# The step-by-step scan of layer 1 moved into array tiles of 32, with its row layout made by DMA

## The chip, the cores and the metric

One program runs on one core of a Trainium2 chip. The metric is the device time of one execution in microseconds, lower is better. Times in a profile are counted from the start of its span.

## The reference

Two layers work on x of 2 batches x 1024 tokens x 256. Layer 0 is a linear attention and a sparse feed-forward; neither is touched here. Layer 1 is a scan and a mixture of eight experts. What is computed in layer 1:

```
h = layernorm(x) * (1 + ca) + sa
k, v = h @ Wk.T, h @ Wv.T            # 16 heads of 16 wide, k gets a rotation by position
for each minibatch of 16 tokens:     # 64 of them, per batch and head; W starts as the identity
    z = k W;   W = W - k.T (z - v) * 2/(16*16)
x = x + ga * (layernorm(z) * gamma + beta) @ Wo.T
h = layernorm(x) * (1 + cb) + sb
gates = softmax of the two largest of h @ gate_w, 0 for the other six experts
x = x + gb * (sum_e gates_e * expert_e(h) + shared(h))
```

The minibatches follow one another: each z needs the W that the last gradient left. The expert biases b2 and the shared bias are added as one product of the gates (with a ninth column of ones) and b2.

## The kernel before, in words

Every engine has its instruction order written out by hand; semaphores say what waits for what. The phases are attention, feed-forward, scan (`scan_phase`) and mixture (`moe_phase`); all engines meet at the end of each.

**Scan.** A chunk is 128 tokens of both batches (`NC` = 8 chunks), and a chunk has `NMB` = 8 steps of 16 tokens. A batch has 256 channels in `KD` = 2 halves of 8 heads, so there are four units, one for each batch and half, each with a W of 128 x 128 that is masked to its diagonal blocks. In a step, for each batch:

1. z: TensorE adds k W into the rows of the step in `z_ps` (line 1545). `k_diag` holds k turned, with zeros around the 16 columns of each step, so that the product has 128 rows and only 16 of them are not zero.
2. u: VectorE takes v - z for all 128 tokens (line 1403).
3. gradient: TensorE adds k.T u to `g_ps` (line 1554). `k_rows` holds k once for each step, with the other rows set to zero; ACT makes these copies (`spread`, line 1254).
4. w: VectorE multiplies `g_ps` by `head_blocks`, the mask times 2/256 (`new_w`, line 1374).

Both batches are in every step, batch 0 first on each engine. In 32-bit float each matrix product is two loads of weights and two matmuls in the profile, which are called records below.

Around the steps stand pieces for the next and the last chunk, each at a fixed place: on TensorE (`filler`) the turning of the normalized x, of k and of z, the projection to k and v (3 pieces for each batch, line 1480), and the output rows (line 1488); on VectorE the norms, the split of h in a high and a low part (`split`, lines 1353 and 1355), the rotation (lines 1365 and 1367), and the gating of the output rows (line 1349). ACT drains turned tiles and keeps v and z; POOL sums the rotation (line 1209), adds to x (line 1214) and computes 1/sqrt. The last chunk also has the norms and the split of the mixture's first group of 512 tokens (lines 204, 220, 1593, 1595).

Behind the last step come the statistics of z (line 1337), its centring, turning and output rows, and then the mixture.

**Mixture.** Four groups of 512 tokens. For each, 16 matmuls of 8 columns give the logits (line 1791), VectorE picks the top two, TensorE turns the gates (line 1798), which have nine columns, and for each tile of 128 tokens come the product of nine rows of gates with b2 (line 1819), the shared products (line 1821) and eight expert products (line 1833), which VectorE adds up one by one (line 1754). The hidden layer of the next group (line 1808) stands between them.

## Time and profile before

| what | us |
|---|---|
| median of 3 runs | 1100.81 (1100.41 to 1100.9) |
| profiled execution, its own time | 1098.78 |
| its span | 1097.0 |
| from the end of the feed-forward to the scan's first product | 712.3 to 722.2 |
| the scan's 64 steps | 722.2 to 918.5 |
| from the last u to the mixture | 918.5 to 929.5 |
| the mixture | 929.5 to 1097.0 |
| TensorE busy | 1019.1 (93%) |
| VectorE busy | 733.8 (67%) |

The profile is of one execution. Its own time and its span differ by what lies before the first and behind the last instruction. PE is TensorE's matmuls, PEld its loads of weights, DVE is VectorE; a queue's name has a q at its end.

### The profile page before, as it was taken

The numbers are of one execution on the slowest core, as the hardware profiler recorded it, in microseconds if no ns is written. First come the engines' busy times: TensorE is split into PE (matmuls) and PEld (weight loads), VectorE is DVE, ScalarE is ACT, GpSimd is POOL, SyncE is SP. The second block draws the span as 40 slices with busy tenths as digits, with TensorE's granted clock in tenths as the row PEclk, the third lists the DMA queues.
The fourth block names the chain that finished last, engine by engine and source line by source line (L and its number), as shares of the span: only waits on it lengthen the run. The fifth ranks groups of instructions, "written<-read, shape, count | busy, mean of one in ns | idle before, by whom it ended". The sixth has DMA issues, their size and how long they took to land. (4 is left out here: it accounts for less than half of the span.)

```text
span 1097.0 us, 15610 instructions
## 1 busy us (share of the span) xinstructions
PE 1019.1 (93%) x5736; PEld 850.5 (78%) x5736; DVE 733.8 (67%) x1657; ACT 380.9 (35%) x731; POOL 227.2 (21%) x284
## 2 busy tenths in 40 slices
PE   6899999999999999998699999888999887999997
PEld 5688888888888888887588888667777775877775
DVE  7766667666666676666569866577878775466456
ACT  4334333333434333333133222044455433421220
POOL 2222222222222221222110011132222224111011
PEclk9999999999999999999999999999999998999999
DMA  9300000000000000000130000030000000000000
GB/s 302 110 1 1 1 1 1 1 1 1 1 1 1 1 1 1 1 1 16 33 100 1 1 1 1 0 98 0 0 0 0 1 2 1 1 15 15 10 20 19
DMA packets 19058, 20.91 MB, mean 19 GB/s; under 512 B 4905, under 2 KB 14898, under 8 KB 18994
## 3 DMA queue, kind: packets, MB, share of 16 engines
q1 hardware_dynamic: 18994, 20.05, 5.6%
q8 instruction: 41, 0.67, 0.3%
q14 instruction: 23, 0.19, 0.1%
HBM read 17.95 MB, written 2.10 MB: 18 GB/s over the span
## 5 line engine op out<-in xcount | busy, mean ns | idle before, releaser
L393 POOL TENSOR_TENSOR rope_sum<-rope_cos,rope_sin 128x512 f32<-128x512 f32 x80 | 115.0, 1437 | 257.0 <-DVE rope_sin L514 257.0
L429 ACT ACTIVATE rope_exp<-rope_sum 128x512 f32<-128x512 f32 x80 | 50.5, 631 | 205.7 <-POOL rope_sum L393 205.6
L783 PE MATMUL proj<-wo_sb,attn_out_t 128*128 128x256 f32 x512 | 113.2, 379 | 0.7 <-issue 0.7
L783 PEld LDWEIGHTS proj<-wo_sb,attn_out_t 128*128 128x128 f32 x512 | 96.1, 190 | 13.4 <-issue 0.9
L732 PE MATMUL num<-v_ones,score_masked 128*128 128x129 f32 x512 | 100.2, 278 | 5.9 <-DVE score_masked L572 5.9
L1754 DVE SCALAR_TENSOR_TENSOR m_acc<-m_expert,gates,m_acc 128x256 f32<-128x256 f32 x128 | 61.9, 484 | 58.6 <-PE m_expert L1833 52.1
L733 PE MATMUL num<-state,q_t 128*128 128x129 f32 x512 | 99.9, 277 | 0.0
L732 PEld LDWEIGHTS num<-v_ones,score_masked 128*128 128x128 f32 x512 | 83.0, 193 | 13.4 <-DVE score_masked L572 8.0
L511 DVE TENSOR_TENSOR rope_cos<-proj,cos_sb 128x512 f32<-128x512 f32 x80 | 55.3, 691 | 52.6 <-PE proj L686 52.6
L1554 PE MATMUL g_ps<-t_u,k_rows 128*128 128x128 f32 x512 | 72.7, 284 | 17.2 <-DVE t_u L1403 16.4
L1554 PEld LDWEIGHTS g_ps<-t_u,k_rows 128*128 128x128 f32 x512 | 63.4, 191 | 31.0 <-DVE t_u L1403 27.8
L686 PE MATMUL proj<-w_hi,a_h_hi 128*128 128x512 f32 x192 | 79.3, 494 | 3.9 <-DVE w_lo L136 2.2
L733 PEld LDWEIGHTS num<-state,q_t 128*128 128x128 f32 x512 | 78.6, 194 | 0.0
L1374 DVE TENSOR_TENSOR t_w<-g_ps,head_blocks 128x256 f32<-128x256 f32 x130 | 55.1, 425 | 30.6 <-PE g_ps L1554 29.0
L1545 PE MATMUL z_ps<-t_w,k_diag 128*128 128x128 f32 x512 | 71.5, 282 | 2.5 <-ACT t_z L1325 1.3
L526 DVE SCALAR_TENSOR_TENSOR feat<-rope_sum,rope_exp 128x512 f32<-128x512 f32 x80 | 69.1, 864 | 6.9 <-ACT rope_exp L431 6.9
L1545 PEld LDWEIGHTS z_ps<-t_w,k_diag 128*128 128x128 f32 x512 | 63.9, 191 | 9.4 <-DVE t_w L1374 3.9
L1254 ACT ACTIVATE k_rows<-t_k,rows_of 128x256 f32<-128x256 f32 x128 | 54.3, 509 | 45.3 <-POOL t_k L1209 45.3
L1833 PE MATMUL m_expert<-w_sb,m_act 128*128 128x256 f32 x256 | 67.7, 407 | 2.1 <-DVE m_acc L1754 2.1
L724 PE MATMUL score<-q_t,k_t 128*128 128x512 f32 x128 | 66.9, 605 | 0.0
L714 PEld LDWEIGHTS turn<-ident,feat 128*128 128x128 f32 x320 | 38.1, 142 | 32.3 <-issue 25.8
L1072 PE MATMUL f_rows<-wd_sb,hidden 128*128 128x256 f32 x256 | 58.1, 380 | 5.4 <-DVE f_dx L991 2.9
(205 smaller groups left out, 1993.4 us busy)
## 6 DMA issues: line engine op xcount, KB each, us to landing
a_stage<-in_wqkv SPq DMA_DIRECT2D x6, 512.0 KB, 5.4
wo_sb<-in_wo SPq DMA_DIRECT2D x1, 2048.0 KB, 10.1
a_stage<-in_wgu SPq DMA_DIRECT2D x4, 512.0 KB, 9.2
out<-x_sb SPq DMA_DIRECT2D x16, 128.0 KB, 1.7
x_sb<-in_x SPq DMA_DIRECT2D x2, 768.0 KB, 11.5
f_wmod<-in_wmod SPq DMA_DIRECT2D x1, 1536.0 KB, 9.0
w_sb<-in_w SPq DMA_DIRECT2D x1, 1280.0 KB
a_wmod<-in_wmod SPq DMA_DIRECT2D x1, 1024.0 KB, 6.5
```

Of the source, the lines that this page charges most:

```text
L393: pool.tensor_tensor(y[:, parity], t1[:, parity], t2[:, parity], ALU.add).then_inc(s["y_done"], 1)
L526: dve.scalar_tensor_tensor(dst, y[:, parity], 0.0, ex[:, parity], ALU.max, ALU.add).then_inc(s["feat_done"], 1)
L686: mm = pe.matmul(proj[:, bank, :], hh[:, parity, k, :], ww[:, k, cols], start=(i == 0 and k == 0), stop=(i == 2 and k == KD - 1))
L724: pe.matmul(score[:, g % 2, :], k_t[:, g, :], q_t[:, g, :], start=True, stop=True).then_inc(s["score_full"], 1)
L732: pe.matmul(dst, am[:, g % 2, r * P:(r + 1) * P], v[:, b, g, :], start=True, stop=False)
L733: mm = pe.matmul(dst, q_t[:, g, r * P:(r + 1) * P], state[:, b, g, :], start=False, stop=True)
L783: mm = pe.matmul(proj[:, b, 0:D], o_t[:, i, :], wo[:, i, :], start=(i == 0), stop=(i == H - 1))
L1072: mm = pe.matmul(rows[:, n % 2, 0:D], hid[:, g % 2, m, i * P:(i + 1) * P], wd[:, m, :], start=(m == 0), stop=(m == NM - 1))
L1545: mm = pe.matmul(z_ps[:, b, k * P:(k + 1) * P], k_diag[:, b, k, n * P:(n + 1) * P], w[:, b, k], start=(n == 0 and k == 0), stop=(n == NMB ...
L1554: mm = pe.matmul(g_ps[:, b, k * P:(k + 1) * P], k_rows[:, b, n, k * P:(k + 1) * P], u[:, b, k * P:(k + 1) * P], start=False, stop=False, s ...
L1754: ins = dve.scalar_tensor_tensor(acc[:, n % 2], expert[:, k % 2, j * D:(j + 1) * D], gates[:, g % 2, i, e:e + 1], acc[:, n % 2], ALU.mult, ...
L1833: mm = pe.matmul(expert[:, k % 2, j * D:(j + 1) * D], act_t[:, g % 2, e, toks], w2[:, e, :], start=True, stop=True)
```

## The change

The four units of a step are worked together, each in its own quarter of TensorE's array.

- **z** (`values`): four products with 32 columns of weights (`k_t`, k turned, the step's 16 columns and the next 16) and 128 rows, into partitions 32 j to 32 j + 31 of `z_ps` for unit j. The products of units 0 and 1 wait for the first masking only.
- **u** (`residual`): one operation of 128 x 128 for all four units, in rows: partition 32 j + s is token s of the step in unit j.
- **gradient** (`gradient`): four products of 16 rows, at partitions 32 j, into a bank each of `g_ps`.
- **w** (`new_w`): two operations of 128 x 256, one for each batch, as before, but from four banks and in one function for all units.
- **Row layout**: k and v of a chunk go to memory and come back as rows of the units (`kv_rows`: for each batch one transfer out, two in); u goes out in four transfers and comes back in two, as tokens (`u_rows_out`), and POOL then forms z = v - u (`keep_z`). All are issued by SP. The first residual of a chunk waits for the transfers of k and v.
- `k_diag`, `k_rows`, `spread` and `spread_blocks` fall away. The split of h moves from VectorE to ACT (`high`) and POOL (`low`).
- The pieces beside the steps have new places: at most one between two operations of the chain (`beside_g` and `beside_z` on VectorE, `beside_u` and `beside_w` on TensorE). The output rows of a chunk come two chunks later, in halves. The loop over chunks is written out in place of a hardware loop.
- **Mixture**: the gates have 128 columns in place of nine, with zeros behind the ninth, and b2 has 128 rows, with zeros behind the ninth.

```diff
...
-            ("w2_sb", [P, NH, D]), ("b1_sb", [P, NH]), ("b2_sb", [E + 1, D]), ("gate_w_sb", [P, KD, E]))]
+            ("w2_sb", [P, NH, D]), ("b1_sb", [P, NH]), ("b2_sb", [P, D]), ("gate_w_sb", [P, KD, E]))]
...
-            kr, v = sb("t_k", [P, B, D]), sb("t_v", [P, B, D])
-            STEP = P + MB
-            k_diag = sb("k_diag", [P, B, KD, NMB * STEP])
-            k_rows = sb("k_rows", [P, B, NMB, D])
...
+            kv = sb("t_kv", [P, 2, B, KD, 2, P])
+            k_t = sb("k_turned", [P, 2, U * P + MB])
+            kv_r, u_r = sb("kv_rows", [P, 2, NMB, 2, P]), sb("u_rows", [P, 2, NMB, P])
+            u_tok = sb("t_u", [P, B, D])
+            w = sb("t_w", [P, U, P])
...
+            kv_ps = ps("kv_ps", [P, B, 512])
+            turn, z_ps = ps("t_turn", [P, 512]), ps("z_ps", [P, 512])
+            g_ps = ps("g_ps", [P, U, 512])
+            kv_dram = nc.dram_tensor("kv_scratch", (2, B, P, KD * 2 * P), F32, kind="Internal").ap()
+            u_dram = nc.dram_tensor("u_scratch", (2, B, P, D), F32, kind="Internal").ap()
...
+                def kv_rows(c, b):
+                    q = c % 2
+                    sp.wait_ge(kr_done, nth(b, c + 1))
+                    sp.wait_ge(v_kept, nth(b, c + 1))
+                    sp.dma_start(kv_dram[q, b], kv[:, q, b].rearrange("p k u e -> p (k u e)")).then_inc(kv_out[b], 16)
+                    if c >= 2:
+                        sp.wait_ge(g_full, 1 + (c - 1) * NMB)
+                        sp.wait_ge(u_done, (c - 1) * NMB)
+                    sp.wait_ge(kv_out[b], 16 * (c + 1))
+                    for k in range(KD):
+                        src = kv_dram[q, b].rearrange("(n s) (k d) -> k s n d", n=NMB, k=KD)[k]
+                        sp.dma_start(kv_r[unit(b, k), q].rearrange("s n u e -> s n (u e)"), src).then_inc(kv_in[b], 16)
+
+                def u_rows_out(c):
+                    q = c % 2
+                    sp.wait_ge(u_done, (c + 1) * NMB)
+                    for b in range(B):
+                        for k in range(KD):
+                            dst = u_dram[q, b].rearrange("(n s) (k d) -> k s n d", n=NMB, k=KD)[k]
+                            sp.dma_start(dst, u_r[unit(b, k), q]).then_inc(u_out[b], 16)
+                    for b in range(B):
+                        if c:
+                            sp.wait_ge(z_kept, nth(b, c))
+                        sp.wait_ge(u_out[b], 16 * KD * (c + 1))
+                        sp.dma_start(u_tok[:, b], u_dram[q, b]).then_inc(u_in[b], 16)
+
+                sp.wait_ge(zeroed, 1)
+                for b in range(B):
+                    kv_rows(0, b)
                 w2, b1, b2, gw = self.moe_small
                 sp.dma_start(gw[:], a["gw"].rearrange("(k p) n -> p k n", p=P)).then_inc(self.moe_in, 16)
                 sp.dma_start(b1[:], a["b1"]).then_inc(self.moe_in, 16)
...
-                sp.dma_start(w2[:], a["w2"].rearrange("(m p) n -> p m n", p=P)).then_inc(self.moe_in, 16)
-                for i in range(3):
-                    w = min(WCH, NH * P - i * WCH)
-                    self.load_chunk(sp, NCH + i, a["w1"][:, i * WCH:i * WCH + w], w)
+                sp.wait_ge(zeroed, 3)
+                sp.dma_start(b2[0:E + 1, :], a["b2"]).then_inc(self.moe_in, 16)
...
+                def low(c, b):
+                    pool.wait_ge(hi_done, nth(b, c + 1))
+                    pool.tensor_tensor(h_lo[:, b], h[:, b], h_hi[:, b].bitcast(F32), ALU.subtract).then_inc(hl_done, 1)
+
+                def keep_z(c, b):
+                    pool.wait_ge(u_in[b], 16 * (c + 1))
+                    if c:
+                        pool.wait_ge(zn_done, nth(b, c))
+                    pool.tensor_tensor(zs[:, b].rearrange("p (k e) -> p k e", k=KD), kv[:, c % 2, b, :, 1],
+                                       u_tok[:, b].rearrange("p (k e) -> p k e", k=KD), ALU.subtract).then_inc(z_kept, 1)
...
-                def spread(c, b, j, waited=True):
-
-                    if waited:
-                        act.wait_ge(g_full, nth(b, c * NMB + (j - NMB + 2)))
-                    act.activation(k_rows[:, b, j], kr[:, b], ACT.Copy, scale=rows_of[:, j:j + 1]
-                                   ).then_inc(k_rows_done, 1)
...
+                def high(c, b):
+                    act.wait_ge(h_done, nth(b, c + 1))
+                    if c:
+                        act.wait_ge(proj_full, nth(b, c))
+                    act.activation(h_hi[:, b], h[:, b], ACT.Copy).then_inc(hi_done, 1)
...
 
...
+                def residual(c, n):
+                    i = c * NMB + n
+                    dve.wait_ge(z_full, i + 1)
+                    if n == 0:
+                        for b in range(B):
+                            dve.wait_ge(kv_in[b], 16 * KD * (c + 1))
+                            if c >= 2:
+                                dve.wait_ge(u_out[b], 16 * KD * (c - 1))
+                    dve.tensor_tensor(u_r[:, c % 2, n], kv_r[:, c % 2, n, 1], z_ps[:, 0:P], ALU.subtract).then_inc(u_done, 1)
+
+                def new_w(i):
+
+                    dve.wait_ge(g_full, i + 1)
+                    for b in range(B):
+                        mine = slice(b * KD, (b + 1) * KD)
+                        dve.tensor_tensor(w[:, mine], g_ps[:, mine, 0:P], blocks[:].unsqueeze(1).broadcast_to([P, KD, P]),
+                                          ALU.mult).then_inc(w_done[b], 1)
...
-                def split(b, n):
-                    dve.wait_ge(h_done, nth(b, n))
-                    dve.tensor_copy(h_hi[:, b], h[:, b]).then_inc(hi_done, 1)
-                    dve.wait_ge(hi_done, nth(b, n))
-                    dve.tensor_tensor(h_lo[:, b], h[:, b], h_hi[:, b].bitcast(F32), ALU.subtract).then_inc(hl_done, 1)
...
+                    def beside_g(n):
+                        if n == 0 and ahead:
+                            x_norm(dve, c + 2, 0)
...
+                    def beside_z(n):
+                        if n == 0 and ahead:
+                            x_norm(dve, c + 2, 1)
...
+                    for n in range(NMB):
+                        residual(c, n)
+                        beside_g(n)
+                        if c * NMB + n + 1 < NC * NMB:
+                            new_w(c * NMB + n + 1)
+                        beside_z(n)
...
+                def values(c, n):
+
+                    if n == 0:
+                        pe.wait_ge(kt_done, nth(1, c + 1))
+                        if c == 0:
+                            pe.wait_ge(zeroed, 2)
+                    for j in range(U):
+                        if j % KD == 0:
+                            pe.wait_ge(w_done[j // KD], c * NMB + n + 1)
+                        col = j * P + n * MB
+                        mm = pe.matmul(z_ps[UP * j:UP * (j + 1), 0:P], k_t[:, c % 2, col:col + UP], w[:, j],
+                                       start=True, stop=True)
+                    mm.then_inc(z_full, 1)
+
+                def gradient(c, n):
+
+                    pe.wait_ge(u_done, c * NMB + n + 1)
+                    if n == 0:
+                        for b in range(B):
+                            pe.wait_ge(kv_in[b], 16 * KD * (c + 1))
+                    for j in range(U):
+                        rows = slice(UP * j, UP * j + MB)
+                        mm = pe.matmul(g_ps[:, j, 0:P], kv_r[rows, c % 2, n, 0], u_r[rows, c % 2, n],
+                                       start=False, stop=False, skip_group_check=True)
                     mm.then_inc(g_full, 1)
-                for b in range(B):
...
+                norm_turn(1)
+
+                for c in range(NC):
+                    prev, nxt, ahead = c > 0, c + 1 < NC, c + 2 < NC
+
+                    def beside_u(n):
+                        if n in (0, 1, 2) and nxt:
+                            project(c + 1, n // 2, (0, 2, 1)[n])
+                        if n in (3, 4) and c >= 2:
+                            out_rows(c - 2, n - 3, 0)
+                        if n == 5 and nxt:
+                            k_turn(c + 1, 0)
+                        if n == 5 and not nxt:
+                            self.turn_group(pe, 0, kv_ps)
+                        if n == 7 and ahead:
+                            norm_turn(c + 2)
+
+                    def beside_w(n):
+                        if n in (0, 1, 2) and nxt:
+                            project(c + 1, (n + 1) // 2, (1, 0, 2)[n])
+                        if n in (3, 4) and c >= 2:
+                            out_rows(c - 2, n - 3, 1)
+                        if n == 5 and nxt:
+                            k_turn(c + 1, 1)
+                        if n == 7 and prev:
+                            out_turn(c - 1)
...
+                        values(c, n)
+                        beside_u(n)
+                        gradient(c, n)
+                        beside_w(n)
...
-            gates_t = sb("gates_t", [E + 1, 2, GT, P])
+            gates = sb("gates", [P, 2, GT, P])
+            gates_t = sb("gates_t", [P, 2, GT, P])
...
-                    act.activation(gates_t[:, g % 2], small[0:E + 1, :].rearrange("p (i t) -> p i t", i=GT), ACT.Copy
+                    act.activation(gates_t[:, g % 2], small[:].rearrange("p (i t) -> p i t", i=GT), ACT.Copy
...
-                dve.memset(gates[:], 1.0)
+                dve.memset(gates[:], 0.0).then_inc(s["gate_step"], 1)
+                dve.wait_ge(s["gate_step"], 1)
+                dve.memset(gates[:, :, :, E:E + 1], 1.0)
...
-                        t = pe.transpose(small[0:E + 1, i * P:(i + 1) * P], gates[:, g % 2, i, :], ident[:])
+                        t = pe.transpose(small[:, i * P:(i + 1) * P], gates[:, g % 2, i, :], ident[:])
                     t.then_inc(s["gturn_full"], 1)
...
```

## Rows read from the trace of the kernel before

**Rows 1.** Busy time by stage: stretch, its length, engines, granted clock, DMA.

```profile
722.20:918.50 196.30, 175.48 (x1250) 152.73 (x1249) 152.94 (x414) 90.74 (x232) 47.02 (x85) 1.00 0.01 2
918.50:929.50 11.00, 6.09 (x20) 4.07 (x20) 4.18 (x13) 2.33 (x6) 3.63 (x7) 0.69 0.00 0
929.50:1097.00 167.50, 158.11 (x696) 122.86 (x696) 94.91 (x283) 40.85 (x67) 20.51 (x28) 0.96 0.04 13
```

**Rows 2.** Timeline of the scan: start, duration, engine, line, tiles, shapes, count, idle.

```profile
785.43 0.71 PE L1480 MATMUL t_proj<-w_lo,t_h_hi 128*128 128x512 f32 x2
...
792.40 0.87 DVE L1374 TENSOR_TENSOR t_w<-g_ps,head_blocks 128x256 f32<-128x256 f32 x2 [0.47 <-PE g_ps L1554]
...
792.88 1.16 PE L1545 MATMUL z_ps<-t_w,k_diag 128*128 128x128 f32 x8
...
793.63 0.87 DVE L1403 TENSOR_TENSOR t_u<-t_v,z_ps 128x256 f32<-128x256 f32 x2
...
794.10 1.16 PE L1554 MATMUL g_ps<-t_u,k_rows 128*128 128x128 f32 x8
...
794.85 0.87 DVE L1374 TENSOR_TENSOR t_w<-g_ps,head_blocks 128x256 f32<-128x256 f32 x2 [0.36 <-PE g_ps L1554]
```

**Rows 3.** Groups by line and shape, whole span: busy us, mean ns, idle before.

```profile
L1403 DVE TENSOR_TENSOR t_u<-t_v,z_ps 128x256 f32<-128x256 f32 x128 | 50.2, 417 | 12.7 <-PE z_ps L1545 10.8
...
L1465 PEld LDWEIGHTS t_turn<-ident,t_zn 128*128 128x128 f32 x32 | 3.9, 149 | 3.5 <-DVE t_zn L1344 3.5
...
L1798 PEld LDWEIGHTS m_small<-ident,gates 128*9 128x9 f32 x16 | 1.4, 90 | 0.9
...
L1732 DVE TENSOR_TENSOR picked<-lane,top_at_f 128x32 f32<-128x32 f32 x8 | 1.1, 184 | 0.0
```

**Rows 4.** Timeline, VectorE in the last step: the split of the first group.

```profile
915.58 1.35 DVE L1593 CAST m_h_hi<-m_h 128x1024 fp32r<-128x1024 f32 x1
...
916.96 1.63 DVE L1595 TENSOR_TENSOR m_h_lo<-m_h,m_h_hi 128x1024 fp32r<-128x1024 f32 x1
```

**Rows 5.** Timeline, TensorE around one nine-row product of the mixture.

```profile
958.83 0.62 PE L1808 MATMUL m_hid<-m_h_lo,w_hi 128*128 128x512 f32 x2
959.38 0.29 PEld L1819 LDWEIGHTS m_shared<-b_sb,gates_t 9*128 9x128 f32 x2 [0.36 <-issue]
...
960.00 0.73 PEld L1821 LDWEIGHTS m_shared<-w_sb,m_act 128*128 128x128 f32 x4 [0.33 <-issue]
...
960.97 1.24 PE L1833 MATMUL m_expert<-w_sb,m_act 128*128 128x256 f32 x5
```

**Rows 6.** The stores of the result: ns to issue, and us to landing.

```profile
L1646 SPq DMA_DIRECT2D out<-x_sb x16: 332/332/366, 960.6 to 1094.9; - x16
...
DMA to landing us min/median/max: 1.7/1.7/3.0
```

**Rows 7.** Timeline, where the scan's steps begin and where they end.

```profile
721.26 0.72 POOL L1209 TENSOR_TENSOR t_k<-t_rope_cos,t_rope_sin 128x256 f32<-128x256 f32 x1 [0.58 <-DVE t_rope_sin L1367]
...
722.96 0.42 DVE L1403 TENSOR_TENSOR t_u<-t_v,z_ps 128x256 f32<-128x256 f32 x1 [1.12 <-PE z_ps L1545]
...
918.51 0.74 DVE L1403 TENSOR_TENSOR t_u<-t_v,z_ps 128x256 f32<-128x256 f32 x2
...
920.51 0.75 DVE L1337 BATCH_NORM_STATS2 t_stats<-t_z 128x6 f32<-128x256 f32 x2
```

**Rows 8.** Timeline, eight expert records at two places of the mixture.

```profile
956.18 1.89 PE L1833 MATMUL m_expert<-w_sb,m_act 128*128 128x256 f32 x8
...
992.40 3.50 PE L1833 MATMUL m_expert<-w_sb,m_act 128*128 128x256 f32 x8
```

**Rows 9.** Busy time and granted clock (third number from the end) of three stretches.

```profile
715.00:716.00 1.00, 0.00 (x0) 0.00 (x0) 0.94 (x1) 0.73 (x3) 1.00 (x1) 1.00 0.92 98
...
990.00:992.00 2.00, 2.00 (x13) 1.60 (x14) 0.00 (x0) 0.00 (x0) 0.45 (x1) 1.00 0.00 0
...
993.00:995.00 2.00, 2.00 (x6) 1.55 (x6) 0.73 (x2) 0.00 (x0) 0.00 (x0) 0.50 0.00 0
```

More of the change, by code:

```diff
@@ new lines, in _ @@
+                    if prev:
+                        for b in range(B):
+                            z_rstd_of(c - 1, b)
+                    if c >= 2:
+                        for b in range(B):
+                            add_rows(c - 2, b)
+                    if ahead:
+                        for b in range(B):
+                            low(c + 2, b)
+                    if not nxt:
+                        for i in range(3):
+                            self.chunk_low(pool, NCH + i, i * WCH, min(WCH, NH * P - i * WCH))
@@ L1381, in _ @@
                     x_aggregate(dve, b)
+                new_w(0)
+                dve.wait_ge(xn_turned, nth(1, 1))
                 for b in range(B):
[L1383 to L1385 removed]
                     x_centre(dve, 1, b, 2)
@@ L1495, in _ @@
                     mm.then_inc(g_full, 1)
-                for b in range(B):
-                    norm_turn(b, 1)
+                for j in range(U):
+                    mm = pe.matmul(g_ps[:, j, 0:P], ident[:], ident_n[:], start=True, stop=False, skip_group_check=True)
+                mm.then_inc(g_full, 1)
+                norm_turn(0)
                 for b in range(B):
                     for i in range(3):
-                        project(b, 1, i)
+                        project(0, b, i)
@@ L1566, in turn_group @@
+                for c in (NC - 2, NC - 1):
+                    if c == NC - 1:
+                        out_turn(c)
+                    for b in range(B):
+                        for k in range(KD):
+                            out_rows(c, b, k)
     def turn_group(self, pe, g, turn):
```

437 lines of the change are left out of this document (193 added, 244 removed).

## The prediction, made before the changed kernel ran

> **What bounds the kernel now.** I read the page's head, then the busy time by stage, then one step of the scan in the timeline, then the two ends of the scan and one row of the mixture. The profiled execution took 1098.78 us of its own time, 1.78 more than its span of 1097.0, where the last stage of [rows 1] ends; the sum below is made against 1098.78, and the median of the runs shown, 1100.81, lies 2.03 above that.
>
> The scan's steps fill 722.2 to 918.5, 196.3 us for 64 steps, 3.07 each [rows 1]. The reader is to see that TensorE (175.5 busy) and VectorE (152.9) are both nearly full there: the two batches are worked in turn, so that one engine has a batch while the other has the other one. In the timeline of a bare step [rows 2] w is masked from 792.40, z's eight records (each matrix product is two) begin at 792.88, u follows at 793.63, the gradient's eight at 794.10, and the next masking at 794.85: 2.45 us. Eight records from a standstill take 1.16; four are answered by VectorE after 0.75 (794.10 to 794.85), so a further record costs 0.10 to 0.11; I use 0.11. The other 0.6 of the mean step is side work between the steps. Behind the steps the scan has 11.0 us more, and the mixture 167.5, in which TensorE is 158.1 busy [rows 1].
>
> **The step after the change.** It is one chain for all four units, no longer two in turn. Its parts:
> - two maskings of 128x256: 0.87, as now [rows 2], and 0.05 until TensorE starts (793.63 + 0.42 to 794.10 shows that size of gap);
> - z of units 2 and 3, since that of 0 and 1 was begun under the second masking. Four records in a row are 0.75. No row shows products in different parts of the array, so bounds: one after another 0.75, all units beside each other 0.53 (a unit's own two records still follow each other). In between: the last record of a unit beside the first of the next, 0.64. I take that, because records start in program order in every row, and a unit's second needs the rows that its first streams. The load is of 32 columns: a load of 9 columns takes 90 ns where one of 128 takes 149 [rows 3], so 0.06 less: 0.58;
> - one residual of 128x128 in place of two of 128x256. 128x256 is 417 ns, 128x32 is 184 [rows 3], by the line between them 0.29, and 0.05 to TensorE: 0.34;
> - the gradient's eight records: in a row 0.75 + 4 x 0.11 = 1.19, beside each other 0.53, paired 0.86, which I take.
>
> Sum 0.87 + 0.05 + 0.58 + 0.34 + 0.86 = 2.70; with no overlap 3.14, with full overlap 2.26. 64 steps: 172.8 (201 or 145).
>
> **Side work.** VectorE's pieces (0.42 each) now stand one at a time in the waits for TensorE (0.58 and 0.86) and cost nothing; where TensorE became faster (0.47 and 0.53) they would still just fit. The splitting of h leaves VectorE for ACT and POOL, which have room (90.7 and 47.0 busy of 196.3) [rows 1]; the eight spreading copies a chunk of k for each batch leave ACT. TensorE's pieces cost more than now. A projection piece is 0.71 from a standstill (785.43) [rows 2]; beside the residual it has 0.34, and some 0.14 of its start and end overlap its neighbours, so 0.23 is late; beside the maskings next to nothing, 0.03. With three of each a chunk, two halves of the output rows on each side at the same price, and 0.2 for the four transposes of x: 1.5 a chunk, 12 in all. The last chunk has the mixture's first group on VectorE (split 1.35 + 1.63 in one piece [rows 4], norms and centring) in waits that hold 0.6: 4. Steps and side work: 172.8 + 12 + 4 = 188.8 against 196.3: **7.5 less**.
>
> A row shows what a change of shape costs TensorE: the load of the nine-row product waits for the matmul before it, and the next full load waits 0.33 again [rows 5]. In the scan most such changes fall where TensorE waits for VectorE anyway; the rest is in the 0.71 above. The Trainium skill has the rule (TensorEngine Tiling, Key Properties: a change of tiling mode, not of tile, drains TensorE); the trace agrees. If each of the four changes of a step had to be paid on the chain, the step would be 1.3 longer, which I exclude, as a drained array has nothing to drain.
>
> **The row layout by DMA.** Inside, it has time: k and v of a chunk are ready about half a chunk (12 us) ahead, the four transfers one behind another take about 8 us. At the ends it is bare. A store of 128 KB lands 1.7 us after its issue (1.7 to 3.0), an issue holds SP for 0.33 to 0.37 [rows 6]. At the start, k of batch 1 is summed at 722.0 and the first u runs at 722.96 [rows 7]. After: the splitting on POOL comes behind a fill and delays batch 0's k to about 721.3; out 2.1, two in issued 0.7, then batch 1's out 2.1 and in 2.4 (it stands behind batch 0 on SP): 728.6, and 0.6 for 256 KB: the first residual at 729.2 to 729.5. **6.5 more**, bounds 5 and 11. VectorE has it at the head of its queue, so everything behind it waits too.
>
> At the end, u goes out (four issues, 1.4, landing 1.7), comes in (0.7 + 1.7), and POOL forms z (0.73 a batch): batch 0's at 6.05 after the last residual, batch 1's at 6.8. Now z's statistics start at 920.51, 1.26 after the last u [rows 7]. **5.2 more**, bounds 4 and 8. Nothing covers it: the mixture starts only when all engines are through.
>
> **The mixture.** With 128 rows in place of nine the shape does not change. From 958.83, where a full-width pair starts, to 960.97, where the expert products start, are 2.14 us [rows 5]. With no stop: 0.47 for the pair and six records at 0.216 ((1.89 - 0.38) / 7 [rows 8]) = 1.77. Saves 0.37, 16 times: 5.9, on TensorE where it is the bound, and in the last group too, where shared and expert products stand between two runs of VectorE. Second: three times eight expert records took 3.5 (992.40) where they take 1.89 [rows 8]; the granted clock there is 0.50 [rows 9], 1.2 GHz in place of 2.4. Ahead of it TensorE did 16 matmuls of only eight columns and then the nine-row product. If the padded product holds the clock, 3 x 1.6 = 4.8. Bounds 0 and 4.8; taken whole. **10.7 less**, bounds 5 and 11. The wider gate tiles cost nothing: the copy of the gates is as long in its free size.
>
> **Sum.** -7.5 + 6.5 + 5.2 - 10.7 = -6.5: 1092.3 of its own time, 1094.3 as a median.
>
> **Rivals.**
> - *The clock falls in the scan* (slower). For: 1.0 turned to 0.5 behind narrow and nine-row products although TensorE counts as fully busy [rows 9]; the new step is made of products that use a quarter of the array, and steps 5 and 6 of a chunk have almost no full-size side work. Against: from 715 to 716 TensorE did nothing at all, and the clock stayed at 1.0 [rows 9]. Price: at half clock a record of 256 columns costs 0.2 more [rows 8], one of 128 0.1, so a step some 0.8 and its side work 0.2 more. One to two such steps a chunk: +8 to +20, 1102 to 1114, likeliest 1107; in all steps +64. It decides from about seven slow steps on.
> - *No overlap in the array* (slower): the fp32 loads or the order of records keep the tiles apart. Every row of now shows strict 0.11 spacing, for it and against nothing. 64 x 0.44 = +28: 1122; if only the gradient's 128-column loads stay apart, +21: 1115.
> - *Full overlap* (faster): 64 x 0.44 = -28, of which some 5 come back as TensorE's side work gets shorter cover: 1071. For it speaks only that the four units share no operand. The Trainium skill (TensorE: Matmul & The Clock Gate, Part 3) reports four row tiles at 3.07 times the speed of one after another, for 512 columns. No run here shows it; by it the sum would be near this rival's 1071.
> - *The mixture's clock gain does not come*: +4.8, 1099. It lies inside the range.
> - *A transfer comes late in each chunk*: needs the chain of four transfers at 12 us in place of 8; then +1 to +4 a chunk. Under 0.05.
>
> **How the numbers follow.** Paired overlap at full clock 0.37; clock 0.27; no overlap 0.18; full overlap 0.18. Paired at full clock has its own range 1085 to 1103. A difference under 0.2% (2.2 us) can't be told from no change. Faster: 0.30 of the first, all of full overlap, 0.02 of the clock: 0.50. Same: 0.06 + 0.05: 0.11. The rest, 0.39, is slower. The range leaves out the far half of full overlap and of the dearest clock cases: 1070 to 1122.
>
> **What would show it.** In the changed profile: a bare step of 2.7 from one masking to the next, with z records of 128x32 and gradient records of 16 rows; the gradient's eight records in 0.86 to VectorE's answer (0.53 or 1.19 in the rivals); the granted clock 1.00 throughout the scan (rival: 0.5 in stretches, once or more a chunk, behind step 4); the first residual near 729; statistics of z 6 us behind the last residual; no gap on either side of the shared product and eight expert records at 1.9 after each logits. The prediction fails if the bare step is above 2.9 or below 2.5, or if side work holds the chain by over 3 us a chunk.

## The result, and the profile after

| kernel | median of its runs, us | ratio to before, 95% interval |
|---|---|---|
| before (4 runs) | 1100.61 (1098.85 to 1100.9) | |
| changed (4 runs) | 1128.74 (1126.41 to 1131.27) | 1.0259 (1.0234 to 1.0285) |

The change makes the kernel 2.6% slower: 28 us, where 6.5 less was forecast, and outside the forecast's range. The profiled execution took 1129.39 us (span 1127.3) against 1098.78. First the page of the changed kernel: TensorE's busy share in 40 slices, and its granted clock.

```profile
PE 1036.0 (92%) x5736; PEld 801.3 (71%) x5736; DVE 687.1 (61%) x1560; ACT 331.8 (29%) x603; POOL 249.1 (22%) x318
...
PE   6899999999999999997899998588999985899997
...
PEclk9899999999999999999999999855555556799999
```

The reader is to see the row of fives: the clock is at its lower level, 1.2 GHz, through nearly the whole scan, while the busy share there is eight and nine tenths. The windows by stage (stretch, length, busy time of PE, PEld, DVE, ACT, POOL, granted clock, DMA share, GB/s) are the wait for the first rows, the steps, the tail behind the last residual, and the mixture:

```profile
723.90:732.20 8.30, 1.82 (x11) 0.71 (x10) 0.01 (x1) 1.55 (x5) 1.45 (x2) 0.50 0.53 98
732.20:943.50 211.30, 190.52 (x1222) 95.85 (x1222) 106.20 (x320) 37.35 (x93) 60.68 (x108) 0.51 0.27 65
943.50:965.00 21.50, 10.21 (x32) 7.00 (x32) 5.86 (x13) 3.01 (x8) 9.36 (x13) 0.64 0.12 25
965.00:1127.30 162.30, 152.14 (x696) 125.88 (x696) 95.75 (x284) 40.90 (x67) 20.50 (x28) 0.96 0.04 14
```

Against [rows 1] and [rows 7] the 30.3 us more of span are these:

| stretch | before | after | difference | forecast |
|---|---|---|---|---|
| up to TensorE's first matmul in the scan phase | 712.8 | 713.1 | +0.3 | 0 |
| from there to the first residual (722.96, 732.19) | 10.2 | 19.1 | +8.9 | +6.5 |
| first to last residual | 195.6 | 211.3 | +15.8 | -7.5 |
| last residual to the mixture | 11.1 | 21.5 | +10.4 | +5.2 |
| mixture | 167.4 | 162.3 | -5.1 | -10.7 |

The lengths are starts to starts; before, the residuals are those of batch 0. The numbers are rounded one by one.

**The steps.** A bare step at the lower clock (timeline; one masking to the next, 2.72 us):

```profile
768.90 0.76 DVE L1406 TENSOR_TENSOR t_w<-g_ps,head_blocks 128x256 f32<-128x256 f32 x2 [0.60 <-PE g_ps L1597]
...
769.38 0.97 PE L1585 MATMUL z_ps<-t_w,k_turned 128*32 128x128 f32 x8 [0.55 <-DVE t_w L1406]
...
770.40 0.29 DVE L1399 TENSOR_TENSOR u_rows<-kv_rows,z_ps 128x128 f32<-128x128 f32 x1 [0.41 <-PE z_ps L1585]
...
770.74 0.81 PE L1597 MATMUL g_ps<-u_rows,kv_rows 16*128 16x128 f32 x8 [0.39 <-DVE u_rows L1399]
...
771.62 0.76 DVE L1406 TENSOR_TENSOR t_w<-g_ps,head_blocks 128x256 f32<-128x256 f32 x2 [0.61 <-PE g_ps L1597]
```

The same in the last chunk, where eight full-width transposes stood ahead and the granted clock was 1.00 from 935 to 938 (2.18 us):

```profile
935.83 0.76 DVE L1406 TENSOR_TENSOR t_w<-g_ps,head_blocks 128x256 f32<-128x256 f32 x2 [1.52 <-PE g_ps L1597]
...
937.10 0.29 DVE L1399 TENSOR_TENSOR u_rows<-kv_rows,z_ps 128x128 f32<-128x128 f32 x1
...
937.44 0.50 PE L1597 MATMUL g_ps<-u_rows,kv_rows 16*128 16x128 f32 x8 [0.39 <-DVE u_rows L1399]
...
938.01 0.76 DVE L1406 TENSOR_TENSOR t_w<-g_ps,head_blocks 128x256 f32<-128x256 f32 x2 [0.29 <-PE g_ps L1597]
```

A step with projection pieces on both sides, at the lower clock: 3.63 from 896.43 to 900.06. The pair of the piece alone is 1.22 and starts as soon as z is through; u is ready at 898.46 (898.17 + 0.29), and the gradient doesn't begin before 899.18:

```profile
896.43 0.76 DVE L1406 TENSOR_TENSOR t_w<-g_ps,head_blocks 128x256 f32<-128x256 f32 x2 [1.61 <-PE g_ps L1597]
...
898.03 1.22 PE L1563 MATMUL kv_ps<-w_lo,t_h_hi 128*128 128x512 f32 x2
898.17 0.29 DVE L1399 TENSOR_TENSOR u_rows<-kv_rows,z_ps 128x128 f32<-128x128 f32 x1 [0.65 <-PE z_ps L1585]
...
899.18 0.81 PE L1597 MATMUL g_ps<-u_rows,kv_rows 16*128 16x128 f32 x8
...
900.06 0.76 DVE L1406 TENSOR_TENSOR t_w<-g_ps,head_blocks 128x256 f32<-128x256 f32 x2 [1.27 <-PE g_ps L1597]
```

**The start.** SP's queue and the first residual (timeline):

```profile
721.68 0.34 SPq L1191 DMA_DIRECT2D kv_scratch<-t_kv  x1
723.71 0.81 SPq L1198 DMA_DIRECT2D kv_rows<-kv_scratch  x2
724.63 0.36 SPq L1191 DMA_DIRECT2D kv_scratch<-t_kv  x1
728.08 0.78 SPq L1198 DMA_DIRECT2D kv_rows<-kv_scratch  x2
...
732.19 0.29 DVE L1399 TENSOR_TENSOR u_rows<-kv_rows,z_ps 128x128 f32<-128x128 f32 x1 [10.73 <-DMA kv_rows<-kv_scratch]
```

Batch 1's store took 3.45 here, in flight beside batch 0's loads (batch 0's took 2.03), and the last load landed some 3.3 behind its issue. The page's DMA issues (count, KB each, median us from issue to landing) point the same way: 128 KB into 16 partitions take 3.5, where a store of 128 KB takes 1.7 in [rows 6] and u coming back over 128 partitions 2.0. Whether the few partitions or the transfers in flight beside them make the difference, no run here separates.

```profile
kv_rows<-kv_scratch SPq DMA_DIRECT2D x32, 128.0 KB, 3.5
u_scratch<-u_rows SPq DMA_DIRECT2D x32, 64.0 KB, 2.2
t_u<-u_scratch SPq DMA_DIRECT2D x16, 128.0 KB, 2.0
```

**The end** (timeline). VectorE's split takes 3.24 beside POOL's subtractions (L136, three in a row from 939.73), where it took 1.63 in [rows 4] beside POOL's additions to x; u's stores keep SP for 3.05; z's statistics start 7.09 behind the start of the last residual, and behind them POOL first adds the output rows of the chunk before (L1268, 952.89) and takes 1/sqrt only then (L1253, 954.25).

```profile
939.73 7.34 POOL L136 TENSOR_TENSOR w_lo<-t_stage,w_hi 128x1024 fp32r<-128x1024 f32 x3
940.35 3.24 DVE L1679 TENSOR_TENSOR m_h_lo<-m_h,m_h_hi 128x1024 fp32r<-128x1024 f32 x1
943.52 0.28 DVE L1399 TENSOR_TENSOR u_rows<-kv_rows,z_ps 128x128 f32<-128x128 f32 x1
...
943.82 3.05 SPq L1206 DMA_DIRECT2D u_scratch<-u_rows  x4
...
947.65 1.23 SPq L1211 DMA_DIRECT2D t_u<-u_scratch  x2
...
950.61 0.43 DVE L1411 BATCH_NORM_STATS2 t_stats<-t_z 128x6 f32<-128x256 f32 x1 [4.66 <-POOL t_z L1248]
...
952.89 1.41 POOL L1268 TENSOR_TENSOR x_sb<-x_sb,t_dx 128x256 f32<-128x256 f32 x2 [1.49 <-DVE t_dx L1428]
954.25 0.19 POOL L1253 TENSOR_TENSOR t_veps<-t_mv,eps 128x1 f32<-128x1 f32 x1
```

The Trainium skill (GPSIMD Engine Reference, Specifications) says that POOL shares its SBUF interfaces with VectorE, with contention when VectorE's instruction has two inputs in SBUF. By that rule the two slow each other; the trace agrees (3.24 beside POOL), and experiment 8 below has 1.23 with POOL out of the way. It also shows that the cost only moved.

**The mixture** (timeline). No stop is left on either side of the shared product, and the eight expert records behind the logits take 1.89 at full clock in place of the 3.50 of [rows 8]:

```profile
989.92 0.68 PE L1905 MATMUL m_shared<-b_sb,gates_t 128*128 128x256 f32 x2
...
990.43 1.03 PE L1907 MATMUL m_shared<-w_sb,m_act 128*128 128x256 f32 x4
...
991.30 1.89 PE L1919 MATMUL m_expert<-w_sb,m_act 128*128 128x256 f32 x8
```

But its first 10 us run at the lower clock now (granted clock 0.54 from 965 to 975; before 1.00 from 929.5 to 939.5).

### The profile page after: what moved, and what is told of

It reads as the page before. It is cut to its first block and busy times, and to the rows that moved or that the text cites. A ratio compares the mean times of both kernels' runs of the same rounds, so it can differ in the third digit from the quotient of the medians.

```text
span 1127.3 us, 15207 instructions
## 1 busy us (share of the span) xinstructions
PE 1036.0 (92%) x5736; PEld 801.3 (71%) x5736; DVE 687.1 (61%) x1560; ACT 331.8 (29%) x603; POOL 249.1 (22%) x318
## 3 DMA queue, kind: packets, MB, share of 16 engines
q1 hardware_dynamic: 32818, 32.64, 10.4%
## 5 line engine op out<-in xcount | busy, mean ns | idle before, releaser
L1406 DVE TENSOR_TENSOR t_w<-g_ps,head_blocks 128x256 f32<-128x256 f32 x128 | 48.4, 420 | 68.5 <-PE g_ps L1597 68.4
L1597 PEld LDWEIGHTS g_ps<-u_rows,kv_rows 16*128 16x128 f32 x512 | 32.7, 304 | 51.7 <-DVE u_rows L1399 28.8
L1597 PE MATMUL g_ps<-u_rows,kv_rows 16*128 16x128 f32 x512 | 51.4, 491 | 18.2 <-DVE u_rows L1399 18.2
L1919 PE MATMUL m_expert<-w_sb,m_act 128*128 128x256 f32 x256 | 62.9, 385 | 2.9 <-DVE m_acc L1838 2.9
L686 PE MATMUL proj<-w_lo,a_h_hi 128*128 128x512 f32 x192 | 61.3, 400 | 0.0
L686 PE MATMUL proj<-w_hi,a_h_lo 128*128 128x512 f32 x192 | 61.0, 399 | 0.0
L1072 PEld LDWEIGHTS f_rows<-wd_sb,hidden 128*128 128x128 f32 x256 | 48.2, 190 | 13.9 <-issue 6.0
```

Of the source, the lines that this page charges most:

```text
L686: mm = pe.matmul(proj[:, bank, :], hh[:, parity, k, :], ww[:, k, cols], start=(i == 0 and k == 0), stop=(i == 2 and k == KD - 1))
L1072: mm = pe.matmul(rows[:, n % 2, 0:D], hid[:, g % 2, m, i * P:(i + 1) * P], wd[:, m, :], start=(m == 0), stop=(m == NM - 1))
L1597: mm = pe.matmul(g_ps[:, j, 0:P], kv_r[rows, c % 2, n, 0], u_r[rows, c % 2, n], start=False, stop=False, skip_group_check=True)
L1919: mm = pe.matmul(expert[:, k % 2, j * D:(j + 1) * D], act_t[:, g % 2, e, toks], w2[:, e, :], start=True, stop=True)
```

## The experiments

The "added matmuls" below are products of 384 columns of a piece of w_hi with another, into columns of `z_ps` or `g_ps` that nobody reads. They leave the chain's operands alone and only give TensorE work where it would wait.

**1. Before, with the mixture's padding alone.** The scan is that of before; `gates`, `gates_t` and b2 have 128 columns and rows.

```diff
-            gates_t = sb("gates_t", [E + 1, 2, GT, P])
+            gates_t = sb("gates_t", [P, 2, GT, P])
```

> The kernel before with the mixture's gates and b2 padded to 128 and nothing else. If padding removes both the stops around the nine-row product (0.37 each, 16 times) and the half clock behind the logits (three times 1.6), the time falls by 10.7 us, to about 1090. If only the stops go, by 5.9, to 1095. If padding brings nothing by itself, 1100.6.

Measured: 1091.42 (1090.51 to 1092.93), ratio 0.9919 (0.9892 to 0.9947): 9.6 us less, by the interval 5.8 to 11.9, which alone doesn't tell both parts (10.7) from the stops only (5.9). The profile does: the mixture took 157.2 in place of 167.5, at a granted clock of 0.99 for 0.96, and the expert records behind the logits take 1.89:

```profile
932.00:1089.20 157.20, 147.21 (x696) 121.86 (x696) 95.76 (x284) 40.87 (x67) 20.33 (x26) 0.99 0.04 14
```

So the term of 10.7 holds nearly whole, with both its parts, and the loss is the scan's: alone the scan's part of the change costs some 37 us (1128.74 - 1091.42).

**2. Changed kernel, TensorE kept busy until the first step only.** 14 added matmuls ahead of the turning of k, 4 behind it, 36 in the first step's wait for the rows.

```diff
+                spin(z_ps[:, P:512], 14)
                 for b in range(B):
                     k_turn(0, b)
+                spin(z_ps[:, P:512], 4)
...
+                        if c == 0 and n == 0:
+                            spin(g_ps[:, 0, P:512], 36)
```

> The changed kernel with matmuls whose result nobody reads (384 columns, full array) only around the first transfer: 14 behind the projections, 4 behind the turning of k, 36 while the first residual waits. If the clock is low in the scan because it fell in that wait and the side work can't raise it again, it stays at 1.0 for the scan from here on and the time falls by 35 to 50 us, to about 1085. If the steps themselves are too light for the full clock, it falls within the first chunk or two and the time stays within 5 us of 1128.

In this and the next two kernels the added matmuls in `g_ps` restart unit 0's accumulation, so its W is not the reference's: what is timed has the same instructions, but other numbers in unit 0. Experiment 5 puts that right. Measured: 1126.93 (1125.96 to 1128.05), ratio 1.024 (1.0205 to 1.0276). The clock reached the steps at its full level and fell in them, in the first chunk:

```profile
732.00:740.00 8.00, 7.01 (x64) 3.40 (x64) 5.40 (x18) 0.38 (x1) 2.18 (x5) 1.00 0.08 28
740.00:745.00 5.00, 3.52 (x42) 1.80 (x42) 3.07 (x9) 0.77 (x2) 0.72 (x1) 0.91 0.49 115
745.00:930.00 185.00, 171.94 (x1089) 86.26 (x1086) 90.36 (x282) 34.68 (x88) 51.16 (x94) 0.50 0.29 71
```

So it is not the long wait at the start alone that lowers it; the steps don't hold it. But TensorE also has idle time in them (3.52 busy of 5.00), so this doesn't say yet whether the idle time or the form of the products does it. Experiment 7 does.

**3. The same, with added matmuls in the steps too**: in a bare step 2 beside the residual and 4 beside the masking, with side work 0 and 1.

```diff
                         beside_u(n)
+                        spin(g_ps[:, 0, P:512], 0 if side(c, n) else 2)
                         gradient(c, n)
                         beside_w(n)
+                        spin(z_ps[:, P:512], 1 if side(c, n) else 4)
```

> The same start, and in every step such matmuls beside the chain too: two beside the residual and four beside the masking, where side work stands none and one. If light steps are the cause, the clock stays at 1.0 in most of the scan; the bare step is then some 2.5 to 2.8 (2.18 at full clock plus what these matmuls are late), and the time falls by 25 to 45 us, to 1083 to 1103. If the clock is not what makes the scan long, the matmuls only add to it: 1135 or more.

Measured: 1077.19 (1074.76 to 1078.59), ratio 0.9778 (0.9742 to 0.9813), below even the 1083 that was expected of light steps as the cause. The clock stays at 1.00 from 735 to 890. Work that nobody needs takes 50 us off experiment 2.

**4. The steps' added matmuls without the warm start.**

```diff
-                spin(z_ps[:, P:512], 14)
...
-                spin(z_ps[:, P:512], 4)
...
-                            spin(g_ps[:, 0, P:512], 36)
```

> The same matmuls in every step, but none around the first transfer. If the added work is enough to raise the clock as well as to hold it, it comes up within the first chunk and the time is within 5 us of the run with both. If it only holds it, the clock stays at 0.5 through the scan, the added matmuls take twice as long, and the time is over 1140.

Measured: 1089.51, one run, 12 us above experiment 3 where within 5 was expected. The clock came up at the end of the first chunk and stayed, so the steps with the added matmuls can raise it too. The difference is that first chunk: 30.4 at the lower clock, for 19.0.

```profile
724.00:760.00 36.00, 28.86 (x161) 16.74 (x159) 10.11 (x31) 4.16 (x11) 4.36 (x8) 0.51 0.40 95
760.00:765.00 5.00, 5.00 (x45) 3.21 (x44) 1.67 (x5) 2.34 (x6) 1.48 (x2) 0.81 0.35 61
765.00:895.00 130.00, 129.05 (x1203) 80.26 (x1199) 86.75 (x272) 32.06 (x81) 51.03 (x92) 1.00 0.38 86
```

**5. As 3, with unit 0 left whole.**

The third argument is False where the matmul adds to its columns and doesn't restart.

```diff
-                            spin(g_ps[:, 0, P:512], 36)
-                        spin(g_ps[:, 0, P:512], 0 if side(c, n) else 2)
+                            spin(g_ps[:, 0, P:512], 36, False)
+                        spin(g_ps[0:128, 0, P:512], 0 if side(c, n) else 2, False, 128)
```

> The same added matmuls as in the kernel with the warm start and the per-step work (14 before the turning of k, 4 behind it, 36 beside the first step's wait; then in each bare step 2 beside the residual and 4 beside the masking, in each step with side work 0 and 1), but those beside the residual add to their unused columns in place of restarting the bank, so that unit 0 keeps its accumulation. My theory (the clock is what the scan lost): as before, granted clock 1.00 over the scan, bare step 2.3, time 1073 to 1081. Rival (that kernel was fast because unit 0's product was cut short or its numbers were small): then the steps would be longer here and the time above 1090.

Measured: 1076.0 (1072.28 to 1080.55), ratio 0.9788 (0.9748 to 0.9828), clock 1.00 from 730 to 890, first to last residual 159.1. What experiment 3 shows doesn't hang on unit 0; 2 and 4 have no such repeat.

**6. Half as many added matmuls in the steps.**

```diff
-                        spin(g_ps[0:128, 0, P:512], 0 if side(c, n) else 2, False, 128)
+                        spin(g_ps[0:128, 0, P:512], 0 if side(c, n) else 1, False, 128)
...
-                        spin(z_ps[0:128, P:512], 1 if side(c, n) else 4, True, 128)
+                        spin(z_ps[0:128, P:512], 0 if side(c, n) else 2, True, 128)
```

> Half of the added work: 1 matmul of 384 columns beside the residual and 2 beside the masking in a bare step, none in steps with side work; the same warm start. If the clock asks for a certain amount of work on TensorE, this lies between no added work (clock 0.50 from 745 on, 1127) and the whole (1.00, 1077): I expect parts of the scan at 0.50 and a time of 1085 to 1110. If any full-array matmul between the small ones is enough to hold the clock, 1.00 throughout and 1075, a little below the whole dose. If half is as bad as nothing, 0.50 throughout and 1125.

Measured: 1075.11, one run, which can't be told from experiment 5 (1072.28 to 1080.55). The time is that of the second case and not the 1085 to 1110 that I expected; the clock is between the cases: 1.00 up to 865, then lost in the last chunk, which has no projection (0.54 and 0.50 until the last residual), where the whole number held it up to 890. So in that chunk half as many were not enough. First to last residual 159.8: a chunk in the middle takes 18.8 for 19.7 in experiment 5, the last one 29.0 for 22.3.

**7. As many added matmuls as in 5, but each 32 rows by 32 columns.**

The last argument of `spin` is the number of rows and of columns of weights (`w_hi[0:side, 0, 0:side]`).

```diff
-                        spin(g_ps[0:128, 0, P:512], 0 if side(c, n) else 2, False, 128)
+                        spin(g_ps[0:32, 0, P:512], 0 if side(c, n) else 2, False, 32)
...
-                        spin(z_ps[0:128, P:512], 1 if side(c, n) else 4, True, 128)
+                        spin(z_ps[0:32, P:512], 1 if side(c, n) else 4, True, 32)
```

> As many added matmuls with as many columns (384) in the steps as in the full dose, but each with 32 rows and 32 columns of weights, so that it uses one tile of the array; the warm start keeps its full-size matmuls. Theory A (what counts is how much of the array works): the clock falls to 0.50 in the first chunk and stays there, 1120 to 1135. Theory B (what counts is that columns stream, however small the tile): clock 1.00 over the scan, 1073 to 1083.

Measured: 1164.55, one run, 89 us above experiment 5. Theory A; the time is above its range (1120 to 1135), since at the lower clock the added matmuls lengthen the steps and nothing is given back: first to last residual 249.0, for 211.3 in the changed kernel. The profile shows next to no idle time of TensorE from 735 to 969, neither where the clock fell nor behind it:

```profile
745.00:750.00 5.00, 5.00 (x44) 2.50 (x46) 1.92 (x6) 0.94 (x3) 0.00 (x0) 0.73 0.86 187
...
760.00:969.00 209.00, 208.98 (x1184) 100.81 (x1184) 83.14 (x264) 33.35 (x83) 48.43 (x88) 0.50 0.22 52
```

This is the row that the prediction lacked: with products that use a small part of the array, a busy share of 1 goes with a clock of 0.50. From 735 to 745 the same steps had 10.00 of 10.00 busy at 1.00, so it is not idle time that took the clock away.

**8. Changed kernel, ends in another order, no added matmuls.** Batch 1's last u also goes through ACT's queue (not shown).

```diff
                 for b in range(B):
-                    kv_rows(0, b)
+                    kv_store(0, b)
+                for b in range(B):
+                    kv_rows(0, b, True)
...
                     if not nxt:
                         e_rstd(pool, 0)
+                        for i in range(3):
+                            self.chunk_low(pool, NCH + i, i * WCH, min(WCH, NH * P - i * WCH))
...
                 for b in range(B):
-                    add_rows(NC - 2, b)
-                for b in range(B):
                     z_rstd_of(NC - 1, b)
+                for b in range(B):
+                    add_rows(NC - 2, b)
```

> The changed kernel with no added matmuls, and only its two ends in another order: both batches' k and v are stored before either is loaded back; in the last chunk POOL forms the low parts of w1 ahead of 1/sqrt of the chunk before, so that they don't run beside VectorE's split; behind the last step POOL takes 1/sqrt of z before it adds the output rows of the chunk before; batch 1's u goes through ACT's queue. If the 9.2 and 10.4 us that the two ends cost are the transfers' order and these queues, the first residual comes 3 to 4 us earlier (728.5) and the mixture 4 to 7 us sooner behind the last residual (15 to 17 in place of 21.5): together 1117 to 1122. If the ends are bound by the flight of the transfers themselves, under 3 us in all: 1126 or more. The clock is 0.50 over the scan in both.

Measured: 1124.31 (1123.23 to 1124.92), ratio 1.0216 (1.0193 to 1.0239): 4.4 less than the changed kernel, between the two cases. The first residual came only 1.0 earlier:

```profile
722.59 0.97 SPq L1191 DMA_DIRECT2D kv_scratch<-t_kv  x2
...
724.62 1.75 SPq L1203 DMA_DIRECT2D kv_rows<-kv_scratch  x4
...
731.22 0.29 DVE L1413 TENSOR_TENSOR u_rows<-kv_rows,z_ps 128x128 f32<-128x128 f32 x1 [8.86 <-DMA kv_rows<-kv_scratch]
```

The four loads are issued by 726.37, 2.5 earlier than in the changed kernel, and the last lands 4.85 later, for 3.3 there: together they are slower. The split took 1.23 with POOL done beforehand, 2.0 less, but first to last residual is 211.0 for 211.3: POOL's three subtractions now stand beside VectorE's four normalizations of the mixture's first group (L220), which took 3.18 for 1.38. From the last residual to the mixture 20.0 in place of 21.5: the 1/sqrt came sooner, but z's centring now waited for the output rows of the chunk before, behind an ACT that waited for u's store. My edit made that wait. The mixture took 160.7 for 162.3.

**9. Half the added matmuls up to chunk 6, all in chunk 7, both ends, and 52 more behind the last step** (ACT drains ahead of its wait).

```diff
                     if c == NC - 1:
+                        spin(z_ps[:, P:512], 24)
                         out_turn(c)
+                    spin(z_ps[:, P:512], 9)
...
                             out_rows(c, b, k)
+                spin(z_ps[:, P:512], 10)
```

> The half dose of added matmuls in chunks 0 to 6 and the full dose in chunk 7, where the half dose let the clock go; the two ends in the order of the kernel with only its ends changed, but ACT drains the turned z of the chunk before ahead of issuing batch 1's u; and added matmuls behind the last step too (9 while ACT drains, 24 while u travels, 9, and 10 ahead of the mixture). Theory: the tail of the changed kernel and the mixture's first 10 us run at half clock because TensorE idles there; at full clock the output rows take 1.9 in place of 3.6, twice, and the mixture starts 4 to 5 us better off. Against the full dose in the steps alone (1076.0): end 5 to 10 us less, steps 2 less, start 1 less: 1062 to 1070. Rival (the idle time for u's travel is what costs, the clock there is nothing): 1071 to 1075.

Measured: 1067.09 (1066.49 to 1067.35), ratio 0.9707 (0.9691 to 0.9724), 32 us under the kernel before, and inside what its theory said. From the last residual to the mixture 17.5, the mixture 157.5. The same step with projection pieces on both sides is 2.39 here against 3.63 above:

```profile
791.03 0.76 DVE L1421 TENSOR_TENSOR t_w<-g_ps,head_blocks 128x256 f32<-128x256 f32 x2 [0.68 <-PE g_ps L1612]
...
792.29 0.29 DVE L1414 TENSOR_TENSOR u_rows<-kv_rows,z_ps 128x128 f32<-128x128 f32 x1 [0.18 <-PE z_ps L1600]
...
793.42 0.76 DVE L1421 TENSOR_TENSOR t_w<-g_ps,head_blocks 128x256 f32<-128x256 f32 x2 [0.50 <-PE g_ps L1612]
```

First to last residual is 159.6, no less than in 5 and 6, because of two of its own edits. In the last chunk POOL's subtractions stand beside the normalizations as in 8, and here the four take 5.83; TensorE waits 4.78 for the next masking, the granted clock falls to 0.50 (875 to 880), and the chunk takes 27.7 for 22.3 in experiment 5. And the 36 added matmuls end 1.5 behind the first u, which now comes earlier.

```profile
869.71 5.96 POOL L136 TENSOR_TENSOR w_lo<-t_stage,w_hi 128x1024 fp32r<-128x1024 f32 x3
...
870.31 5.83 DVE L220 TENSOR_SCALAR g_xn<-x_sb,g_mv,g_rstd 128x256 f32<-128x256 f32 x4
```

**10. The same, with batch 1's first loads in ACT's queue.**

```diff
                 for b in range(B):
                     keep_k(0, b)
+                act.wait_ge(kv_out[1], 16)
+                for k in range(KD):
+                    src = kv_dram[0, 1].rearrange("(n s) (k d) -> k s n d", n=NMB, k=KD)[k]
+                    act.dma_start(kv_r[unit(1, k), 0].rearrange("s n u e -> s n (u e)"), src).then_inc(kv_in[1], 16)
```

> The same, and the first chunk's two loads of batch 1's rows are issued by ACT's queue, beside SP's two for batch 0. In the kernel with only its ends changed the four issues took 1.75 on SP and the last landed 4.9 us behind its issue. If the issues in one queue are what makes it late, the first residual comes 0.9 to 2 us earlier and the time is 1 to 2 us less than with one queue. If the transfers' own flight into 16 partitions each (4.9) is, no difference: within 0.5 us at the first residual.

Measured: 1070.73 (1068.56 to 1071.6), ratio 0.9736 (0.972 to 0.9752), slower than 9. From the first issue of a store to the first residual it was 8.73 against 8.50 in 9, so the queue of the issues is not what makes it late. What it cost is that ACT stood behind its wait for the store, TensorE behind ACT for 2.3 us, and the clock was 0.66 from 727 to 732; the 36 added matmuls began 3.3 later in the profile and ran on, in part at the lower clock, so that the first step took 6.43 for 3.61. Of the 4.3 by which the two profiles' spans differ these are 2.8, and 1.3 lay ahead of the scan, where both kernels are the same.

## Why the prediction was wrong

**The step that failed** is the clock in the term of the steps, -7.5, which was summed with the granted clock at 1.00 throughout the scan. Measured are +15.8, with the clock at 0.51. The prediction named the rival ("the new step is made of products that use a quarter of the array"), gave it 0.27, and priced one to two slow steps a chunk. Against it stood "from 715 to 716 TensorE did nothing at all, and the clock stayed at 1.0". That row shows only that this one idle us didn't lower the clock. It says nothing on 64 steps of small products, and the other part of [rows 9], where the clock did fall behind narrow products with TensorE fully busy, was the one that bore on this change. Experiments 2, 5 and 7 settle it for this scan: its small products lose the clock, full-array ones between them hold it, small ones in their place don't, with TensorE just as busy (7 is one run, 89 us away). How much full-array work is enough was not measured beyond 6: half as many held it in all chunks but the last.

**Overlap**: paired was taken, full it was. Eight gradient records are 0.50 at full clock, where "beside each other 0.53" was the bound and a row of them 1.19; masking and z up to the residual 1.27 for 1.50 (of that the two maskings 0.76 for 0.87), residual to gradient 0.34 for 0.34, gradient to masking 0.57 for 0.86. Bare step 2.18; the rival said 2.26. The prediction cited the Trainium skill (TensorE: Matmul & The Clock Gate, Part 3) on row tiles that run beside each other; the trace agrees, in 32-bit float and at 128 columns too, with a smaller gain than the page's 3.07: 0.50 for the 1.16 of eight full-array records, 2.3 times. By the prediction's own price full overlap gave back some 28 us, so the two misses, one to each side, partly cancel in the time.

**The price of the clock.** A bare step costs 0.54 more at the lower clock (0.8 forecast), but one with side work on both sides 1.24 more (3.63 against 2.39; 1.0 forecast for step and side work together): behind u the gradient waits 0.72 for a pair of 1.22, and 0.27 for one of 0.74. First to last residual is 211.3 against 159.8 in experiment 6, so the clock costs some 51.5 in the steps (64 forecast for all steps); experiment 6 also has added matmuls and a last chunk at the lower clock in it, so this is rather low. At full clock the prediction's own sum with full overlap, 188.8 - 28 = 160.8 (165.8 with the 5 that it lets come back), stands near the 159.1 to 159.8 of experiments 5, 6 and 9. That they meet so closely is partly luck, since these hold added matmuls that the sum doesn't.

**Start**: +8.9 for +6.5, inside its bounds of 5 and 11. The terms that were low are the transfers: batch 1's store beside batch 0's loads 3.45 for 2.1, and its loads 4.11 from first issue to the residual (728.08 to 732.19) for 2.4. (The 0.6 that the prediction adds for 256 KB has no row there; stores of 256 KB land in 2.0 in the median here, so 0.3 each over the 1.7 of 128 KB.) Order doesn't mend it (in experiment 8 the residual comes 1.0 earlier, in experiment 10 it comes 0.2 later than in 9, counted from the first store).

**End**: +10.4 for +5.2, outside its bounds of 4 and 8. Up to z's statistics the forecast held: they start 6.8 behind the end of the last residual, for 1.26 before, so 5.5 more. (The terms as written, 1.4 + 1.7 + 0.7 + 1.7 + 0.73, make 6.23 for batch 0 and not 6.05.) What the prediction put at nothing is behind the statistics, some 5.3. 1/sqrt starts 3.64 behind them (950.61 to 954.25) for 1.04 (920.51 to 921.55), since it stands in POOL's queue behind the output rows of the chunk before: 2.6. And both batches' last z go through turning and output rows in one piece, where before batch 0's went ahead: from the first centring to the first gating it is 7.6 (955.11 to 962.72) for 4.2 (922.40 to 926.57); 0.8 of that comes back behind it. The split beside POOL (1.6 more) fell into the last step.

**Mixture**: right in its mechanisms, -9.6 in experiment 1 for -10.7. In the changed kernel only -5.1 came, since it starts at the lower clock; with added matmuls ahead of it, in experiment 9, it takes 157.5 (-10).

**The padding's clock gain** fits the same reading in small: with the nine-row product filled up to 128 rows the clock held (experiment 1). The prediction used it in the mixture, with full price, and didn't carry it over to the scan.

## What to carry to other kernels

Packing small products into tiles of the array shortened them here, and took away the full-array work that had kept TensorE's clock up: look at what form of product every stretch is left with, not at its busy share, and compare the price of the lower clock over the whole stretch with the gain. A few full-size matmuls in waits that are there anyway can pay for themselves many times (here 3 in a bare step: some 50 us, experiment 6 against 2). An operation of POOL that is moved out of the way of one operation of VectorE can stand in the way of the next (experiments 8 and 9): look at all that runs beside its new place. Transfers that are hidden inside a loop are bare at both its ends, and there they should be priced with those that fly beside them.

## What the runs showed that was not expected

- TensorE busy 208.98 of 209 us with the clock at 0.50 throughout (experiment 7).
- VectorE's operations beside POOL's subtractions: the split 3.24 for 1.23, four normalizations 3.18 and 5.83 for 1.38 (experiments 8 and 9).
- Eight gradient records of four units take 0.50 at full clock and 0.81 at half, in 32-bit float with two records a product.
- 128 KB into 16 partitions lands in 3.5 us in the median, with four at once 4.85 behind the end of the last issue; 128 KB over 128 partitions in 2.0 (u coming back).
- A matmul that starts an accumulation in columns of its own also restarts that of other columns of the bank: with the added matmuls of experiments 2 to 4 the output is off by a relative 0.09 to 0.14; with those that add in place of restarting (5) it is not.
